# Spectral mixing over 128 rows: sums and plain weights on one half, differences and mirrored signed weights on the other

## The reference, cut to what matters

```python
# layer 0: x = x + conv(groupnorm(x)), x is (32, 64, 128, 128)
def dht_2d(x):                       # normed Hartley transform of each plane
    result = fft2(x).real - fft2(flip(x)).imag
    return result / norm(result)
def compl_mul2d(x1, x2):             # x1: modes of x (32, 64, 20, 20), x2: weights (64, 64, 20, 20)
    x1n, x2n = _neg_freq(x1), _neg_freq(x2)      # mode (a, b) -> (-a mod 20, -b mod 20)
    t1 = einsum('bixy,ioxy->boxy', x1, x2 + x2n)
    t2 = einsum('bixy,ioxy->boxy', x1n, x2 - x2n)
    return 0.5 * (t1 + t2)
out = idht_2d(pad(compl_mul2d(dht_2d(gn(x))[:, :, :20, :20], weights)))
# layer 1: x = x + sobel_magnitude(groupnorm(x))
```

## Time and profile before

| what | us |
|---|---|
| median of 3 runs | 2347.14 (2346.33 to 2347.58) |
| the profiled execution, its own time | 2346.94 |
| its span in the trace | 2345.1 |
| end of the last full work of `pass1` to the first product (701.4 to 746.9) | 45.5 |
| products (746.9 to 841.7) | 94.8 |
| last product to the first work of `pass2` (841.7 to 861.8) | 20.1 |

### The profile page before, as it was taken

The page is one execution under the profiler, slowest core; times in us unless marked ns, Lnnn a source line. Parts: engine busy times, 40 slices in busy tenths (PEclk is TensorE's granted clock), DMA queues, the critical chain, the costliest instruction groups (busy, mean ns, idle before and its releaser), DMA issues.

```text
span 2345.1 us, 60985 instructions
## 1 busy us (share of the span) xinstructions
PE 2212.0 (94%) x21204; PEld 1627.6 (69%) x21204; DVE 1759.6 (75%) x2670; ACT 1946.7 (83%) x3634; POOL 1602.0 (68%) x923
## 2 busy tenths in 40 slices
PE   5999999999992969999999999999999999999998
PEld 4878887888872956666666666666666666666665
DVE  4888888888872156877886887886787787787777
ACT  5888888888871128899898999998989989989998
POOL 4766666666661127777776777777777777777776
PEclk9999999999995568999999999999999999999999
DMA  7777777777787024666666666666666666666665
GB/s 208 206 199 201 199 201 206 197 205 202 200 201 151 2 73 123 186 187 181 188 183 180 187 180 191 182 186 181 180 180 191 188 184 183 182 187 180 197 188 163
DMA packets 808888, 421.40 MB, mean 180 GB/s; under 512 B 20912, under 2 KB 807344, under 8 KB 807472
## 3 DMA queue, kind: packets, MB, share of 16 engines
q1 hardware_dynamic: 808624, 417.86, 62.7%
HBM read 283.56 MB, written 134.22 MB: 178 GB/s over the span
## 4 chain that ended last, share of the span: by engine, by line
PE 61%; issue 1%; DVE 0%; ACT 0%; POOLq 0%; POOL 0%; DVEq 0%; ACTq 0%
PE g_ps L1080 43%; PE y_ps L1072 10%; PE v_ps L1060 7%; PE v_ps L1048 1%; PE g_ps L1100 0%; ACT coef_t L1189 0%; DVE coef L1249 0%; DVE xbuf L1261 0%; DVE xbuf L1233 0%; POOLq L894 0%; POOL p_lo L1021 0%; ACT g_ps L1154 0%; DVE g_ps L1239 0%; PE y_ps L1100 0%; ACT v_sb L1141 0%
## 5 line engine op out<-in xcount | busy, mean ns | idle before, releaser
L1080 PE MATMUL g_ps<-p_hi,stencil 128*128 128x512 f32 x2048 | 854.8, 417 | 9.5 <-DVE xbuf L1261 7.0
L1021 POOL TENSOR_TENSOR p_lo<-pairs,p_hi 128x1032 fp32r<-128x1032 f32 x256 | 617.1, 2411 | 313.9 <-ACT p_hi L1135 313.9
L1080 PE MATMUL g_ps<-p_lo,stencil 128*128 128x512 f32 x2048 | 820.6, 401 | 0.0
L1080 PEld LDWEIGHTS g_ps<-p_hi,stencil 128*128 128x128 f32 x2048 | 388.5, 190 | 289.5 <-POOL p_lo L1021 140.5
L1016 POOL TENSOR_TENSOR pairs<-xbuf 128x1032 f32<-128x1032 f32 x256 | 488.1, 1907 | 48.6 <-POOL p_lo L1021 30.1
L1239 DVE TENSOR_TENSOR g_ps<-gx,g_ps 128x512 f32<-128x512 f32 x512 | 351.3, 696 | 225.1 <-ACT g_ps L1154 217.0
L1261 DVE SCALAR_TENSOR_TENSOR xbuf<-xbuf,rows,g_ps 128x256 f32<-128x256 f32 x1024 | 436.2, 477 | 83.3 <-ACT g_ps L1160 61.4
L330 POOL TENSOR_TENSOR m_lo<-xbuf,m_hi 128x512 fp32r<-128x512 f32 x256 | 305.6, 1194 | 225.1 <-ACT m_hi L442 224.7
L1080 PEld LDWEIGHTS g_ps<-p_lo,stencil 128*128 128x128 f32 x2048 | 389.3, 190 | 81.8
L1160 ACT ACTIVATE g_ps<-g_ps,rows 128x256 f32<-128x256 f32 x1024 | 408.3, 445 | 27.4 <-DVE g_ps L1239 6.0
L523 DVE TENSOR_REDUCE rows<-square 128x1024 f32 (+1 forms) x256 | 311.0, 1215 | 116.5 <-ACT square L474 116.5
(11 more groups left out here) (125 smaller groups left out, 2328.3 us busy)
## 6 DMA issues: line engine op xcount, KB each, us to landing
xbuf<-x SPq DMA_DIRECT2D x256, 512.0 KB, 5.2
xbuf<-x SPq DMA_DIRECT2D x512, 256.0 KB, 3.1
out<-xbuf SPq DMA_DIRECT2D x512, 256.0 KB, 3.5
wmix<-weights SPq DMA_DIRECT2D x16, 800.0 KB, 18.9
second_sb<-second SPq DMA_DIRECT2D x1, 1230.0 KB, 8.3
mats_sb<-mats SPq DMA_DIRECT2D x1, 704.0 KB, 6.5
first_sb<-first SPq DMA_DIRECT2D x1, 32.0 KB, 5.5
```

What stands on the lines that cost most here:

```text
L1021: nc.gpsimd.tensor_tensor(p_lo[:, r % 2, :, 0:W + 1], pairs[:, r % 2, :, 0:W + 1], p_hi[:, r % 2, :, 0:W + 1].bitcast(FP32), ALU.subtract) ...
L1080: mm = nc.tensor.matmul(g_ps[h][:, axis], stencil[:, m, :], p[:, r % 2, 4 * h:4 * h + 4, o:o + W], start=n == 0, stop=n == len(todo) - 1)
```

## The change

The weights are loaded once, into partitions 0 to 63 alone. The upper half of `wmix` gets a copy with modes and mirrors exchanged and signs set (`mirrors`, `flip`): seven operations a piece over 64 partitions (two of 1368 elements, two of 144, two of 72 and one of 32, 3200 in all). ScalarE makes pieces 0, 1, 2, 5 and 6, DVE piece 7, POOL pieces 4 and 3. `part` makes the operands of one half of the images: the sums on partitions 0 to 63 or the differences on 64 to 127, four operations of 144, 2736, 288 and 64 elements on 64 partitions. POOL makes one of the four, DVE three. A product now contracts 128 rows (sums times plain weights plus differences times mirrored signed weights), has a 128x64 weight and 32 moving columns (both halves of the images, 16 tiles each), and goes to one column half: mode to PSUM partitions 0 to 63, mirror to 64 to 127. Nothing accumulates. Each eviction is split by image half, so it is 4 or 6 copies on 64 partitions, 8 in the last two groups.

```diff
             def weights(n):
                 o = slice(n * WCH, (n + 1) * WCH)
-                for q in range(2):
-                    sp.dma_start(wmix[C * q:C * (q + 1), o], w_i[:, o, :]).then_inc(w_in[n], 16)
+                sp.dma_start(wmix[0:C, o], w_i[:, o, :]).then_inc(w_in[n], 16)
...
+        def flip(scaled_copy, n):
+            o = slice(n * WCH, (n + 1) * WCH)
+            src, dst = (wmix[C * q:C * (q + 1), o].rearrange("p o (a b) -> p o a b", b=MODES) for q in range(2))
+            for d, m, sign in mirrors():
+                last = scaled_copy(dst[:, :, d[0], d[1]], src[:, :, m[0], m[1]], sign)
+            return last
...
+        def part(eng, q, upper):
+            src = grid[C * q:C * (q + 1)]
+            half = slice(C * upper, C * (upper + 1))
+            op = (ALU.add, ALU.subtract)[upper]
...
+                last = eng.tensor_tensor(d, src[:, :, c[0], c[1]], src[:, :, m[0], m[1]], op)
...
         def _(pool):
+            weights(4)
+            pool.wait_ge(pool_flipped, 1)
             pool.wait_ge(scaled, 1)
             pool.wait_ge(act_scaled, 1)
+            part(P, 0, 0).then_inc(parted_pool, 1)
+            pool.wait_ge(parted_pool, 1)
+            weights(3)
...
-            def product(n, q, j, s):
-                part = slice(C * q, C * (q + 1))
-                x = operands(*groups[n][j])[part, 1 - s:3 - s]
-                return nc.tensor.matmul(mix_ps[n % BANKS][part, j], wmix[part, :, a * MODES + b], x,
-                                        start=s == 0, stop=s == 1, skip_group_check=True)
+            def product(n, j, h):
+                k = -a % MODES * MODES + -b % MODES if h else a * MODES + b
+                return nc.tensor.matmul(mix_ps[n % BANKS][C * h:C * (h + 1), j], wmix[:, :, k], operand(a, b),
+                                        start=True, stop=True)
...
         def _(act):
+            weights(0)
             act.wait_ge(root_in, 1)
             nc.scalar.activation(root, arg, ACT.Sqrt, scale=4.0 * NPIX).then_inc(rooted, 1)
...
-            act.wait_ge(differences, 1)
-            nc.scalar.activation(near[:, 2].rearrange("p t a b -> p t (a b)"),
-                                 near[:, 0].rearrange("p t a b -> p t (a b)"), ACT.Copy, scale=-1.0)\
-                .then_inc(parted_act, 1)
+            for n in (1, 2, 5, 6):
+                weights(n)
...
         def _(dve):
+            part(V, 1, 0)
+            part(V, 0, 1)
+            part(V, 1, 1).then_inc(parted_dve, 1)
+            dve.wait_ge(w_in[7], 16)
+            flip(scaled_copy, 7).then_inc(flipped, 1)
```

More of the change, by code:

```diff
@@ L18 @@
-import itertools
 from contextlib import ExitStack
@@ L552, in halves, with mirrors @@
             ((slice(0, h + 1, h), slice(1, h)), (slice(0, h + 1, h), slice(n - 1, h, -1)))]
+def mirrors():
+    n, h = MODES, MODES // 2
+    both = slice(0, h + 1, h)
+    back = [((slice(h + 1, n), slice(0, 1)), (slice(h - 1, 0, -1), slice(0, 1))),
+            ((slice(h + 1, n), slice(1, n)), (slice(h - 1, 0, -1), slice(n - 1, 0, -1))),
+            ((both, slice(h + 1, n)), (both, slice(h - 1, 0, -1)))]
+    return [(d, m, 1.0) for d, m in halves()] + [(d, m, -1.0) for d, m in back] + [((both, both), (both, both), 1.0)]
 def mix(nc, sb, ps, sem, mat, x_p, x_all, xpad, modes, rows, late, small, wmix, w_in, mean1, corner, mscale, x_in):
@@ L567, in mix @@
         pair_ps = ps(ctx, "pair_ps", [128, 2, TILES])
-        mix_ps = [ps(ctx, f"mix_ps{g}", [128, 16, 2, TILES]) for g in range(BANKS)]
+        mix_ps = [ps(ctx, f"mix_ps{g}", [128, 16, B]) for g in range(BANKS)]
         wide_ps = [ps(ctx, f"wide_ps{g}", [128, WIDE, TILE // GPL]) for g in range(2)]
@@ L575, in mix @@
         rooted = sem("m_rooted")
+        flipped = sem("m_flipped")
+        pool_flipped = sem("m_pool_flipped")
         scale_ready = sem("m_scale_ready")
@@ L596, in mix, with operand @@
         spare = rows[:].rearrange("p a t n -> p (a t n)")
[L597 to L601, removed]
+        squares = spare[:, 0:TILES * 120].rearrange("p (t m) -> p t m", t=TILES)
+        operands = x_all[:, 0:B * 202].rearrange("p (q t m) -> p q t m", q=2, t=TILES)
+        main = operands[:, :, :, 0:180].rearrange("p q t (a b) -> p q t a b", b=MODES)
+        own_rows = operands[:, :, :, 180:198].rearrange("p q t (a b) -> p q t a b", a=2)
+        own = operands[:, :, :, 198:202].rearrange("p q t (a b) -> p q t a b", a=2)
         diag = late[:].rearrange("p t m -> p (t m)")[:, 0:2 * 512].rearrange("p (g t n) -> p g t n", g=2, t=WIDE)
         grid = modes[:].rearrange("p t (a b) -> p t a b", b=MODES)
[L605 to L609, removed]
+        def operand(a, b):
+            m = 180 + a // H * (H - 1) + b - 1 if a in (0, H) else (a - 1) * MODES + b
+            return operands[:, :, :, m].rearrange("p q t -> p (q t)")
         groups = [[(a, b) for a in range(3 * r + 1, 3 * r + 4) for b in range(5 * c, 5 * c + 5)]
@@ L621, in evictions @@
         def evictions(n):
[L623 to L638, removed]
+            for q in range(2):
+                dst = grid[C * q:C * (q + 1)]
+                near, far = (mix_ps[n % BANKS][C * h:C * (h + 1)].rearrange("p m (q t) -> p q t m", q=2)[:, q]
+                             for h in range(2))
+                if n < RECTS:
+                    r, c = divmod(n, 4)
+                    a, b = 3 * r + 1, 5 * c
+                    b0 = max(b, 1)
+                    near, far = (v[:, :, 0:15].rearrange("p t (a b) -> p t a b", b=5) for v in (near, far))
+                    yield dst[:, :, a:a + 3, b:b + 5], near
+                    yield dst[:, :, 18 - a:21 - a, 16 - b:21 - b0], far[:, :, ::-1, b0 - b:][:, :, :, ::-1]
+                    if b == 0:
+                        yield dst[:, :, 18 - a:21 - a, 0], far[:, :, ::-1, 0]
+                else:
+                    a = (n - RECTS) * H
+                    yield dst[:, :, a, 1:H], near[:, :, 0:H - 1]
+                    yield dst[:, :, a, H + 1:], far[:, :, 0:H - 1][:, :, ::-1]
+                    yield dst[:, :, a, 0], near[:, :, H - 1]
+                    yield dst[:, :, a, H], far[:, :, H - 1]
         def evicted(eng, n):
@@ L645, in evicted @@
                 eng.wait_ge(dve_out, (n + 1) // 2)
+        def flip(scaled_copy, n):
[8 more added lines that the diff above has]
+            op = (ALU.add, ALU.subtract)[upper]
+            dst = main[half, q], own_rows[half, q], own[half, q]
+            both = slice(0, H + 1, H)
+            (c0, m0), (c1, m1), (c2, m2) = halves()
+            for d, c, m in ((dst[0][:, :, :, 0:1], c0, m0), (dst[0][:, :, :, 1:], c1, m1), (dst[1], c2, m2),
+                            (dst[2], (both, both), (both, both))):
+                last = eng.tensor_tensor(d, src[:, :, c[0], c[1]], src[:, :, m[0], m[1]], op)
+            return last
         @block.sync
@@ L655, in _, with weights, scaled_copy @@
             P = nc.gpsimd
+            def weights(n):
+                def scaled_copy(dst, src, sign):
+                    return P.tensor_scalar(dst, src, sign, None, ALU.mult)
+                pool.wait_ge(w_in[n], 16)
+                flip(scaled_copy, n).then_inc(pool_flipped, 1)
+            weights(4)
+            pool.wait_ge(pool_flipped, 1)
             pool.wait_ge(scaled, 1)
             pool.wait_ge(act_scaled, 1)
[L659 to L668, removed]
+            part(P, 0, 0).then_inc(parted_pool, 1)
+            pool.wait_ge(parted_pool, 1)
+            weights(3)
+            pool.wait_ge(pool_flipped, 2)
             for b, (starts, n, last) in enumerate(batches):
@@ L692, in own_product @@
[L692 to L704, removed]
@@ L706, in run, with own_product @@
-            def run(n, q, item):
-                j, s = item
-                return own_product(n, q, j) if s is None else product(n, q, j, s)
+                k = -a % MODES * MODES + -b % MODES if h else a * MODES + b
+                return nc.tensor.matmul(mix_ps[n % BANKS][C * h:C * (h + 1), j], wmix[:, :, k], operand(a, b),
+                                        start=True, stop=True)
+            def own_product(n, h):
+                a = n - RECTS
+                return nc.tensor.matmul(mix_ps[n % BANKS][C * h:C * (h + 1), H - 1], wmix[:, :, (a * MODES + h) * H],
+                                        own[:, :, :, a, h].rearrange("p q t -> p (q t)"), start=True, stop=True)
@@ L711, in _ @@
             pe.wait_ge(parted_dve, 1)
             pe.wait_ge(parted_pool, 1)
[L713 to L718, removed]
-                    pe.wait_ge(act_out if n % 2 == 0 else dve_out, (n - BANKS) // 2 + 1)
[L720 to L726, removed]
+            pe.wait_ge(flipped, PIECES - 2)
@@ L727, in _ @@
+            pe.wait_ge(pool_flipped, 2)
+            for n in range(GROUPS):
+                if n >= BANKS:
+                    pe.wait_ge(act_out if n % 2 == 0 else dve_out, (n - BANKS) // 2 + 1)
+                for j in range(len(groups[n])):
+                    for h in range(2):
```

(12 more changed lines are left out.)

10 lines of the change are left out of this document (5 added, 5 removed).

## The result

The changed kernel took 2315.64 us (median of 4 runs, 2311.74 to 2325.38) against 2346.73 before: a ratio of 0.9875, 95% interval 0.9857 to 0.9893. It is faster, by 31 us where 51 were forecast, and above the range, which ended at 2306. The profiled execution took 2313.55, 33.4 less than the 2346.94 of before.

A forecast was written before the change was run, and what follows sets the result against it. Mixing was taken as bounded by DMA, then by PE. First product 3.4 us sooner, products 48.4 less, last eviction 1.0 more: -50.8, from 2346.94 to 2296 us, with a range of 2272 to 2306.

The forecast's parts named there:

- `pass2` as long as before: The stage behind mixing: it keeps its instructions and was to take as long as before.
- 2 us of issue time: Ahead of mixing: SP's remaining late issues are out some 2.0 us sooner, so the stage starts near 703.9 instead of 705.9.
- Transfers: Before the first product: six late weight pieces instead of twelve issues, landing near 721; PE's wait for them is gone.
- Stage start, root, scaled modes: Start of mixing: stage at 703.9, root at 710.5 (1.9 us later than before), scaled modes at 715.5.
- The price of GpSimd's copy: POOL's mirrored copies before the first product: 1.2 ns per element, 5.2 us a piece, bounds 4.3 and 8.8.
- Turn-taking: Before the first product: POOL and DVE alternate by whole instructions; 28.0 us of shared work, start at 743.5, 3.4 sooner.
- Products: Mixing's matmuls: 800 instructions at 58 ns with the clock at 0.50, 46.4 us instead of 94.8, 48.4 less.
- the clock's rise: Rival, chance 0.35: the clock rises during the products, which take 30.3 us instead of 46.4; time 2282 us.
- Last eviction: Behind the last product: eight copies in 1.7 us instead of three in 0.64, 1.0 us more.
- weight loads went on overlapping: Rival, chance 0.02: weight loads no longer overlap, each instruction costs at least 196 ns, products 157 us; time 2407 us.
- POOL and DVE did disturb each other: Rival, chance 0.12: they hardly disturb each other before the first product, which comes at 729 to 735; time some 2284 us.
- the old pairs were not one: Rival, chance 0.03: old 64-row products already ran in pairs, a 128-row one takes 118 ns, products 94.4 us; time 2344.

The follow-up runs named there:

- e1: Changed kernel with each piece of weights loaded by two issues of half the output channels, sixteen in all; 2296.48 us, ratio 0.9779.
- e3: Changed kernel with eight more waits on SP, for weights long landed, ahead of the first loads of `pass2`; 2292.95 us.
- e4: Changed kernel with SP's loop of `pass2` written out; 2288.09 us, ratio 0.9746.
- e5: Changed kernel with two more waits on SP ahead of the loop of `pass2`; 2287.59 us in one run.
- e2: Kernel before, with both copies of a weight piece written by one issue over 128 partitions, eight issues in all; 2549.8 us.
- e9: Kernel before, with seventeen one-column fills added on VectorE while it waits for the first product; 2337.22 us, ratio 0.9957.
- e7: Changed kernel with SP's loop of `pass2` written out and the mirrored copy of piece 3 moved from GpSimd to ScalarE; 2281.69 us.
- e8: Changed kernel with SP's loop of `pass2` written out and the mirrored copies of pieces 3 and 4 moved from GpSimd to ScalarE; 2281.24 us.
- e12: Changed kernel with two more waits on SP, each product taking its weights from 64 neighbouring numbers (other values mixed); 2275.86 us in one run.

## Why the prediction was wrong, step by step

- **"`pass2` as long as before"**: the step that failed. It was 14.4 us longer; of the 17.4 us between the forecast 50.8 and the measured 33.4 only the other 3.0 lie ahead of it. A change outside a stage moved two loops of that stage within their programs: SP's to a place where each jump costs a fetch (+24.6; e1, e3, e4, e5, and e2 from the other side), VectorE's away from one (-10.2; e9). The prediction counted the late ones of SP's eight issues that went as 2 us of issue time and asked nothing more of them. Without the gaps the changed kernel takes 2288 to 2293 (e1, which starts later, 2296), inside the range, but in part by luck: the 10.2 us of VectorE's loop stood in no step.
- **Transfers**: right. PE no longer waits for them; the last piece landed at 725.7, not near 721, and nothing waited for it.
- **Stage start, root, scaled modes**: the first work came at 704.6 instead of 703.9 and the root at 709.6 instead of 710.5, with one small VectorE operation held up by GpSimd; a second was held up behind the root, which the step had not counted. The scaled modes came at 717.7 (713.78 + 3.91), not 715.5. The price of GpSimd's copy was mis-sized: 1368 elements took 3.66 us, 2.7 ns each, and one small operation waited 3.20 - 0.17 = 3.0 us for them, so at least 2.2 each. That is about the two-operand rate, 2.3, which was the upper bound; the 1.2 taken lay between the ends.
- **Turn-taking**: right in kind (e7, e8). From 717.7 to the first product at 745.5 are 27.8 us where 28.0 were summed, which is in part luck: piece 3 cost 6.6 (745.4 less 738.8, e7) and not 5.2, the rest 21.2 and not 22.8. The start is 1.4 us sooner than before, not 3.4.
- **Products**: 45.7 us for 46.4, by luck: the step had 58 ns at a clock of 0.50, and most of them took 55 at 1.00. The rival that had chance 0.35, the clock's rise, came true, and its 30.3 us did not, because the 36 ns of the earlier trace rows belong to weights in a row. The 58 lay between two numbers that happen to be near the 55 of the stride: the old products' 59, at 0.50, and the 56 of the earlier trace rows, which were weights in a row. That those 56 belong to the slow clock isn't shown: the profile has 1.00 for that stretch (22.70 to 26.20), and the trace's records of the clock begin at 26.0.
- **Last eviction**: 2.05 us, 1.4 more than before, and it starts 1.4 us behind the last product (at 792.7 instead of 791.3), since VectorE was at a batch's sum; 2.8 in all where 1.0 was forecast.
- **The other rivals**: weight loads went on overlapping (208 ns each, one started every 55 to 57); POOL and DVE did disturb each other; the old pairs were not one.

Sum to the first stencil product: -1.4 - 49.0 (45.8 from 745.5 to 791.3, where 94.8 stood) + 2.8 - 0.2 behind that = -47.8.

## What to carry to other kernels

Count the instructions that an edit adds or takes on every engine, the queue that issues transfers too: a loop further down may come to lie where each jump back costs a fetch, and a stage that nobody touched gets longer. Look for pauses without a releaser that come once a turn, and test with two idle waits or the loop written out before you judge the edit. Of a faster clock expect only what the operand's reading leaves.

## What had not been expected of the hardware

- A jump back on SP costs some 5.4 us or nothing: two instructions moved it from the one to the other (e5).
- During the products on all 128 rows the granted clock went from 0.50 to 1.00; during those on 64 rows, as unbroken, it stayed at 0.50 for 94.8 us. That the rows decide it was not tested by itself.
- With 128x64 weights read 1600 bytes apart a matmul instruction takes 56 ns at 0.50 and 55 at 1.00; with weights in a row, 50 and 29 (e12).
- GpSimd's copy of one operand is no quicker per element (2.7 ns, 1368 elements in 3.66 us) than its product of two (2.3 ns, 960 in 2.23 us).
- The pause behind a jump shows in the trace as packets on the instruction queue: two or more in each of the six, none at e3's six jumps.
